# A quad of heads attended two slots after its scores, FFN four slots sooner, the batch loop written out

## What is computed

```python
q = proj(query, Wk, bk); k = proj(key, Wk, bk); v = proj(values, Wv, bv)
scores = einsum('bhqd,bhkd->bhqk', q, k) / sqrt(dk)
scores_ = softmax(where(allow, scores, NEG)) * allow          # allow: strictly below the diagonal
distcum = cumsum(scores_, -1); disttotal = sum(scores_, -1)
dist_scores = sqrt(clip((disttotal - distcum) * |i - j|, 0))
total_effect = clip(exp(dist_scores * -softplus(gammas)), 1e-5, 1e5)
attn = softmax(where(allow, scores * total_effect, NEG))
x = layer_norm(query + (attn @ v) @ Wo.T + bo)
x = layer_norm(x + relu(x @ W1.T + b1) @ W2.T + b2)
```

## Time and profile before

| | |
|---|---|
| median of 3 runs | 1689.13 us (1682.05 to 1694.72) |
| the profiled execution | 1691.98 us |
| its span, first to last instruction | 1689.0 us |
| busy: PE, DVE, ACT, POOL | 1506.9, 1122.4, 1023.1, 157.9 us |
| mean granted clock of TensorE | 0.953 |

### The profile page before, as it was taken

One profiled execution on the slowest core, in us unless ns is written; L12 is line 12 of the kernel. 1 busy time (PEld: TensorE's weight loads), 2 busy tenths in 40 slices (PEclk: granted clock), 3 DMA queues, 4 the chain that ended last, 5 costly groups with the idle time before them and its releaser, 6 DMA issues.

```text
span 1689.0 us, 36801 instructions
## 1 busy us (share of the span) xinstructions
PE 1506.9 (89%) x13056; PEld 1251.6 (74%) x13056; DVE 1122.4 (66%) x3828; ACT 1023.1 (61%) x2674; POOL 157.9 (9%) x107
## 2 busy tenths in 40 slices
PE   4374879999998999999998999999999999988986
PEld 3353668887887888778887878778787878777874
DVE  6576785867766676757857676775857676673221
ACT  1485766676666577666766667666756667674221
POOL 6323110100000010100000010100001010000000
PEclk9786979999998999999999999999999999999998
DMA  5555324656565475646565475656557465566875
GB/s 187 194 187 182 125 101 162 237 177 224 176 212 170 172 251 172 230 170 216 190 207 191 157 244 175 225 177 207 194 178 243 156 234 189 199 224 232 292 270 191
DMA packets 81243, 334.54 MB, mean 198 GB/s; under 512 B 10256, under 2 KB 10256, under 8 KB 64272
## 3 DMA queue, kind: packets, MB, share of 16 engines
q1 hardware_dynamic: 81040, 331.92, 57.3%
HBM read 306.72 MB, written 25.17 MB: 196 GB/s over the span
## 4 chain that ended last, share of the span: by engine, by line
PE 65%; DVE 15%; DMA 8%; issue 5%; ACT 3%; POOL 1%; SPq 1%; DVEq 0%; POOLq 0%; ACTq 0%
PE bank L200 19%; PE bank L201 17%; PE bank L202 17%; PE bank L384 5%; DMA out<-rows 4%; PE bank L398 3%; DVE w_sb L938 3%; DMA w_ring<-w_split 3%; DVE w_sb L950 2%; DVE w_sb L961 2%; PE bank L418 1%; DVE s_sb L926 1%; PE bank L408 1%; DVE c_lo L889 1%; DMA w_split<-w_ring 1%
## 5 line engine op out<-in xcount | busy, mean ns | idle before, releaser
L200 PE MATMUL bank<-xt_hi,w_ring 128*128 128x256 f32 x1024 | 298.4, 291 | 1.9 <-ACT h_sb L721 1.9
L201 PE MATMUL bank<-xt_lo,w_ring 128*128 128x256 f32 x1024 | 291.2, 284 | 0.0
L202 PE MATMUL bank<-xt_hi,w_ring 128*128 128x256 f32 x1024 | 290.8, 284 | 0.0
L200 PE MATMUL bank<-w_ring,h_hi 128*128 128x512 f32 x512 | 219.0, 428 | 23.3 <-DMA w_ring<-w_split 14.7
L721 ACT ACTIVATE h_sb<-bank,b_col 128x256 f32<-128x256 f32 x256 | 106.9, 468 | 212.4 <-DVE h_lo L1027 110.1
L201 PE MATMUL bank<-w_ring,h_hi 128*128 128x512 f32 x512 | 206.4, 403 | 0.0
L384 PE MATMUL bank<-qk_sb 32*32 32x256 f32 (+7 forms) x4096 | 174.3, 298 | 35.8 <-DVE m L926 35.4
L662 ACT ACTIVATE p_sb<-w_sb,nm 128x32 f32<-128x32 f32 (+7 forms) x512 | 206.1, 411 | 0.0
L202 PE MATMUL bank<-w_ring,h_lo 128*128 128x512 f32 x512 | 205.8, 402 | 0.0
L200 PEld LDWEIGHTS bank<-xt_hi,w_ring 128*128 128x128 f32 x1024 | 196.8, 192 | 11.8 <-issue 7.2
L201 PEld LDWEIGHTS bank<-xt_lo,w_ring 128*128 128x128 f32 x1024 | 196.9, 192 | 1.9
(11 more groups left out here) (120 smaller groups left out, 3018.8 us busy)
## 6 DMA issues: line engine op xcount, KB each, us to landing
w_ring<-w_split SPq DMA_DIRECT2D x128, 1024.0 KB, 4.9
w_ring<-w_split SPq DMA_DIRECT2D x256, 512.0 KB, 4.1
w_split<-w_ring SPq DMA_DIRECT2D x32, 512.0 KB, 3.9
x_raw<-x_t SPq DMA_DIRECT2D x16, 512.0 KB, 5.6
c_raw<-ctx_t SPq DMA_DIRECT2D x16, 512.0 KB, 6.2
u_sb<-x_rows SPq DMA_DIRECT2D x16, 512.0 KB, 5.4
ring_raw<-w SPq DMA_DIRECT2D x32, 256.0 KB, 3.0
out<-rows SPq DMA_DIRECT2D x16, 512.0 KB, 6.1
```

The costliest lines, as they stand in the source:

```text
L200: nc.tensor.matmul(dst, a_hi, b_hi, start=start, stop=False)
L201: nc.tensor.matmul(dst, a_hi, b_lo, start=False, stop=False)
L202: return nc.tensor.matmul(dst, a_lo, b_hi, start=False, stop=stop)
```

## The change

Steps are 0 to 18, all written out, with one stage less: in step i the scores of batch i, its attention for quads 0 and 1, the attention of batch i-1 for quads 2 and 3, projection and norm of i-1, and the FFN of i-2 (pairs 0 and 1 of i-1 in slot 3); `done` finishes batch i-3. Quad c goes through `first_exp`, `running_sums` and `effect` in slot c, through `decayed_scores` and `second_exp` in the next, and is attended in the one after that. `s_sb` and `w_sb` have two places, `h_hi` and `h_lo` two each. The weight rings hold four tiles to split, and later two pairs of W1 and two of W2, which is now read back in pairs. The split of the weights takes slots 0 to 5, and its subtraction moves from POOL to DVE. At the start ACT casts wk, wv and wo, DVE subtracts, and POOL casts the first inputs ahead of most constants. SP issues the store of batch i-3 in slot 1 between two of the weight reads, and the rows of the residual after `shift1`. `squared_softplus` moves into slot 0 of step 0.

The diff, cut to the buffers, the orders of ACT and DVE, and slots 1 and 2 of PE:

```diff
-            ring_raw = tensor("ring_raw", [P, 6, 2, 512], F32, loaded)
+            ring_raw = tensor("ring_raw", [P, 8, 2, 512], F32, loaded)
...
-        w_ring = tensor("w_ring", [P, 6, 2, 512], F32R)
+        w_ring = tensor("w_ring", [P, 8, 2, 512], F32R)
...
-        s_sb = tensor("s_sb", [P, NQ, QW])
-        w_sb = tensor("w_sb", [P, NQ, QW])
+        s_sb = tensor("s_sb", [P, 2, QW])
+        w_sb = tensor("w_sb", [P, 2, QW])
...
-        h_hi, h_lo = (tensor(n, [P, 2, S], F32R) for n in ("h_hi", "h_lo"))
+        h_hi, h_lo = (tensor(n, [P, 2, 2, S], F32R) for n in ("h_hi", "h_lo"))
...
-        def over_batches(engine, step):
-
-
-            def plain(i):
-                step(i, i % 2, i < B, 1 <= i <= B, 2 <= i <= B + 1, 3 <= i <= B + 2, 4 <= i, i + 1 < B)
-
-            for i in range(4):
-                plain(i)
-            with engine.Fori(2, B // 2 - 1) as j:
-                step(j * 2, 0, True, True, True, True, True, True)
-                step(j * 2 + 1, 1, True, True, True, True, True, True)
-            for i in range(B - 2, B + 4):
-                plain(i)
-
...
+        def over_batches(step):
+
+
+
+            for i in range(B + 3):
+                step(i, i < B, 1 <= i <= B, 2 <= i <= B + 1, 3 <= i, i + 1 < B)
+
+        def split_in(n):
+
+            return range(3 * n, 3 * n + 3) if n < 4 else range(2 * n + 4, 2 * n + 6) if n < 6 else ()
...
             def first_exp(i, c):
                 act.wait_ge(nm1_ok, NQ * i + c + 1)
-                if not first(i):
-                    act.wait_ge(p_ok, 16 * (i - 1) + HQ * c + HQ)
+                if NQ * i + c >= 2:
+                    act.wait_ge(p_ok, HQ * (NQ * i + c - 1))
...
             def hidden_high(i, p):
                 g = NP * i + p
                 act.wait_ge(h_ok, g + 1)
-                if p > 0 or not first(i):
-                    act.wait_ge(y_step, 2 * g)
-                nc.scalar.copy(h_hi[:], h_sb[:]).then_inc(h_hi_ok, 1)
+                if g >= 2:
+
+                    act.wait_ge(y_step, g - 1)
+                nc.scalar.copy(h_hi[:, p % 2], h_sb[:]).then_inc(h_hi_ok, 1)
...
+            weight_high(0, wk_hi, wk_raw)
+            weight_high(1, wv_hi, wv_raw)
+            act.wait_ge(col_in, 16 * COLS)
+            act.wait_ge(gam_dve, 1)
+            nc.scalar.activation(g_tmp[:, 1], g_tmp[:, 0], ACT.Exp).then_inc(gam_act, 1)
+            weight_high(2, wo_hi, wo_raw)
+            act.wait_ge(const_ok, CONSTS)
+            value_rows(0, 0)
+            over_batches(step)
...
+            def split_low(f):
+                n = f % 4
+                dve.wait_ge(ffw_hi_ok, f + 1)
+                nc.vector.tensor_tensor(w_ring[:, 2 * n:2 * n + 2, 1], ring_raw[:, 2 * n:2 * n + 2, 1],
+                                        w_ring[:, 2 * n:2 * n + 2, 0].bitcast(F32), ALU.subtract).then_inc(ffw_lo_ok, 1)
...
+                if last:
+                    transposes(i - 1, 3, 0)
+                if now:
+                    scores(i, 1, 0)
+                if ffn:
+                    hidden(i - 2, 4)
+                if last:
+                    transposes(i - 1, 3, 1)
+                if now:
+                    scores(i, 1, 1)
+                if last:
+                    transposes(i - 1, 3, 2)
+                if ffn:
+                    add_hidden(i - 2, 3)
+                if now:
+                    scores(i, 1, 2)
+                if last:
+                    attend(i - 1, 3)
+                if now:
+                    pe.wait_ge(v_ok, RT * i + 2)
+                    queries_keys(i, 2)
+                if ffn:
+                    hidden(i - 2, 5)
+                if last:
+                    pe.wait_ge(qk_ok, min(NQ * i + 3, NQ * B))
+                    project_rows(i - 1, 0)
+                if ffn:
+                    add_hidden(i - 2, 4)
+                if now:
+                    transposes(i, 0, 0)
+                    scores(i, 2, 0)
+                if ffn:
+                    hidden(i - 2, 6)
+                if now:
+                    transposes(i, 0, 1)
+                    scores(i, 2, 1)
+                    transposes(i, 0, 2)
+                if last:
+                    pe.wait_ge(u_ok, RT * (i - 1) + 1)
+                    project_rows(i - 1, 1)
+                if ffn:
+                    add_hidden(i - 2, 5)
+                if now:
+                    scores(i, 2, 2)
+                    if last:
+                        pe.wait_ge(u_ok, RT * i)
+                    else:
+                        pe.wait_ge(qk_ok, NQ * i + 3)
+                    queries_keys(i, 3)
+                    attend(i, 0)
+                if ffn:
+                    hidden(i - 2, 7)
+                    add_hidden(i - 2, 6)
+                if last:
+                    turn_rows(i - 1, 0)
...
+                if last:
+                    turned(i - 1, 2, 0)
+                if ffn:
+                    hidden_high(i - 2, 1)
+                    relu(i - 2, 2)
+                if last:
+                    turned(i - 1, 2, 1)
+                    second_exp(i - 1, 3, 0)
+                    turned(i - 1, 2, 2)
+                    second_exp(i - 1, 3, 1)
+                for f in split_in(NQ * i):
+                    split_high(f)
+                if last:
+                    reciprocals(i - 1, 2)
+                if ffn:
+                    hidden_high(i - 2, 2)
+                if last:
+                    concat_high(i - 1, 2)
+                if now:
+                    first_exp(i, 0)
+                    qk_copy(i, 1)
+                if ffn:
+                    relu(i - 2, 3)
+                if done:
+                    deviation2(i - 3)
+                if now:
+                    value_rows(i, 1)
+                    effect(i, 0)
+                if last:
+                    turned(i - 1, 3, 0)
+                if ffn:
+                    hidden_high(i - 2, 3)
+                    relu(i - 2, 4)
+                if last:
+                    turned(i - 1, 3, 1)
+                if now:
+                    second_exp(i, 0, 0)
+                if last:
+                    turned(i - 1, 3, 2)
+                if now:
+                    second_exp(i, 0, 1)
+                for f in split_in(NQ * i + 1):
+                    split_high(f)
+                if last:
+                    reciprocals(i - 1, 3)
+                if ffn:
+                    hidden_high(i - 2, 4)
+                if last:
+                    concat_high(i - 1, 3)
+                if now:
+                    first_exp(i, 1)
+                    qk_copy(i, 2)
+                if ffn:
+                    relu(i - 2, 5)
+                if now:
+                    effect(i, 1)
+                if now:
+                    turned(i, 0, 0)
+                if ffn:
+                    hidden_high(i - 2, 5)
+                    relu(i - 2, 6)
+                if now:
+                    turned(i, 0, 1)
+                    second_exp(i, 1, 0)
+                    turned(i, 0, 2)
+                    second_exp(i, 1, 1)
+                for f in split_in(NQ * i + 2):
+                    split_high(f)
+                if ffn:
+                    hidden_high(i - 2, 6)
+                if last:
+                    deviation1(i - 1)
+                if now:
+                    first_exp(i, 2)
+                    qk_copy(i, 3)
+                    reciprocals(i, 0)
+                    concat_high(i, 0)
+                if ffn:
+                    relu(i - 2, 7)
+                    hidden_high(i - 2, 7)
+                if now:
+                    effect(i, 2)
+                if last:
+                    rows_high(i - 1, 0)
+                if now:
+                    turned(i, 1, 0)
+                    turned(i, 1, 1)
+                if last:
+                    rows_high(i - 1, 1)
+                if now:
+                    second_exp(i, 2, 0)
+                    turned(i, 1, 2)
+                    second_exp(i, 2, 1)
+                for f in split_in(NQ * i + 3):
+                    split_high(f)
+                if now:
+                    reciprocals(i, 1)
+                    concat_high(i, 1)
+                    first_exp(i, 3)
+                if last:
+                    relu(i - 1, 0)
+                    hidden_high(i - 1, 0)
+                if ahead:
+                    qk_copy(i + 1, 0)
+                if last:
+                    relu(i - 1, 1)
+                if now:
+                    effect(i, 3)
+                if ahead:
+                    value_rows(i + 1, 0)
+            weight_high(0, wk_hi, wk_raw)
+            weight_high(1, wv_hi, wv_raw)
+            act.wait_ge(col_in, 16 * COLS)
+            qk_copy(0, 0)
+            act.wait_ge(gam_dve, 1)
+            nc.scalar.activation(g_tmp[:, 1], g_tmp[:, 0], ACT.Exp).then_inc(gam_act, 1)
+            weight_high(2, wo_hi, wo_raw)
+            act.wait_ge(const_ok, CONSTS)
+            value_rows(0, 0)
```

(100 more changed lines are left out.)

647 lines of the change are left out of this document (193 added, 454 removed).

## The result

The changed kernel takes 1736.65 us (median of 4 runs, 1733.75 to 1737.55), the kernel before 1687.41 us in runs beside them (4 runs). The ratio is 1.0299, 95% interval 1.0271 to 1.0326: 3% slower. The forecast was 1715. It had the direction right and the size about half: some 26 us lost (1.5%) were forecast, 49 were measured.

The account below looks back on a forecast made before the run. TensorE was taken to bound the kernel before (91.8 us a batch, 96.2 looped), an ACT and DVE circle the changed one. 190 + 14 x 100.0 - 4 + 68 + 58 = 1712, plus 3: 1715 us, range 1645 to 1758.

Parts of the forecast that it names:

- The circle: Each slot: effect, decayed scores, second exp, first exp, running sums wait in turn across ACT and DVE; at least 18.13 us.
- extras: Other work and waits that the queues put into the circle: 4.6, 6.6, 7.1, 7.9 us in slots 0 to 3.
- The step: One batch in the changed kernel: 98.7 us from the circle, 100.0 with GpSimd and clock; bounds 97 and 103.4.
- GpSimd's 0.6 us: Loss of DVE a step beside GpSimd's input casts and bias add, with one cast meeting running sums.
- no full block: Reading of a scan beside GpSimd's split, 3.77 us against 2.58 alone, used to keep GpSimd's cost at the low end.
- TensorE's idle time: Waits of PE before `attend` in slot 1 and 3 to 4 us at the head of slot 3.
- The 0.7 us: Slot 3: PE's clock drops behind its idle time, later add_hidden and scores move the first exp by this much.
- The head: Stretch up to the first FFN matmul: 190 us against 237.7, bounds 182 and 202.
- The end: Interval to the last batch's FFN 68 us, and last stretch 58 us against 67.5 before.
- The first term: Loop gone and store of `out` issued earlier: at most 4.4 us a batch, 62 us in all.
- rival 3: The circle with 99.5 to 102 us a step, 1707 to 1743 us, slower, the forecast itself; 45%.
- Rival 1: PE stays the bound because the circle fits: 92 to 94 us a step, 1621 us, 4% faster; 10%.

Follow-up runs that it names:

- experiment 2: Changed kernel with `finish_rows` directly behind the running sums of slot 1, ahead of decayed scores, and the store of `out` later in SP's order: 1712.21 us, ratio 1.0143.
- experiment 9: Changed kernel with the orders of TensorE, ScalarE and VectorE rewritten, decayed scores ahead of masks, same operations: 1651.93 us, ratio 0.9781.
- experiment 3: Changed kernel with queries_keys in one pass instead of three, products with the low parts left out: 1727.45 us, ratio 1.0229.
- experiment 4: Changed kernel with GpSimd's add of the bias `bo` cut to 4 elements of a row, so the result lacks `bo`: 1727.12 us, ratio 1.0235.
- Experiment 1: Changed kernel with `finish_rows` moved behind decayed scores and the two masks of slot 1 on DVE: 1723.01 us, ratio 1.0202.
- experiment 10: experiment 9 with slot 3's scores ahead of the FFN's last hidden piece, the second turn_rows behind the last scores, and other moves: 1610.52 us, ratio 0.9545.
- experiment 5: Kernel before with its loop written out and nothing else changed: 1667.29 us, ratio 0.9876.
- experiment 6: Kernel before with its loop written out and the store of `out` issued two pairs earlier in SP's order: 1638.04 us, ratio 0.9697.
- experiment 7: experiment 6 with the start changed: ACT casts weights, DVE subtracts, GpSimd casts inputs before long memsets, TensorE's first projection skips the constants' wait: 1631.36 us, ratio 0.9672.

## Why the prediction was right, and where it was off

**The circle** decided, as the prediction said. Its bare sum of 18.13 us and its extras gave 22.7, 24.7, 25.2 and 26.0 for the slots, before GpSimd and the clock; measured are 22.69, 24.58, 26.27 and 27.60. (The extras listed for slots 2 and 3 add up to 7.0 and 8.0, not 7.1 and 7.9; the two slips cancel.) The start of decayed scores in slot 1, forecast 4.9 us behind `effect`, came at 4.92. Experiments 2 and 9 show it by moving work out of it, experiment 3 by taking TensorE's work away in vain. TensorE is no bystander, though: DVE and ACT wait for it within the circle (0.41 us in slot 0, 2.25 in slot 3, and 2.71 in slot 1 once `finish_rows` is out of the way), and two thirds of what experiment 4 freed went to such a wait. Experiment 1 shows that the count has to follow a moved step to its new place.

**The step** was forecast at 100.0 and took 101.0. The term that was mis-sized is GpSimd's 0.6 us: the rows give 2.3. I had argued that one cast meets running sums; in fact all three operations of a batch meet work of the circle, the casts in slot 2 (1.11 us) and the add in slot 3 (1.15). With them the count gives 26.3 and 27.2 for these slots, against 26.27 and 27.60. The 2.3 is what DVE's own rows lose; removing the add's part brought only 0.4 to 0.5 us a step (experiment 4).

I had also read the row behind this term wrongly, as "no full block". The Trainium skill ("SBUF — State Buffer", SBUF: two separate sides) has the shared port pair held for the whole of an instruction, with the other engine blocked until then. The trace agrees: `hidden_low` ended 0.55 us after the add in fourteen batches of fourteen. In the kernel before, GpSimd's split ran until 60.63 and the scan that began at 59.30 ended 2.43 us after it, about its length alone (2.58). The 1.2 us lost there are the 1.3 us that were left of the split, and not a sign of a milder rule. Nor does the block cost GpSimd's whole 5.1 us a step: what counts is what is left of each operation when one of DVE's begins.

**TensorE's idle time** came where it was said: 1.50 us before `attend` in slot 1 and, at the head of slot 3, more than the 3 to 4 forecast, with the clock at its lower level behind it (1.09 us for a group of four transposes that takes 0.60 to 0.63 at the higher one):

```profile
951.97 0.70 PE L409 MATMUL bank<-zi_wide,head_ones 128*128 128x256 f32 x2 [1.50 <-ACT pt_sb L656]
...
994.32 1.09 PE L399 MATMUL bank<-ident,p_sb 128*128 128x128 f32 x4 [4.90 <-ACT pt_sb L656]
...
1004.71 0.37 ACT L662 COPY cc_sb<-bank 128x256 f32<-128x256 f32 x1 [2.25 <-PE bank L422]
```

It comes back into the circle: ACT then waits 2.25 us for `attend` ahead of the first exp of slot 3, which starts 3.8 us behind the second exp and not 2.9. The 0.7 us that the prediction put down for the clock stands for this wait; how much of it is the clock, no run shows.

**The head** ended at 197.4, not 190. The first `effect` ended at 44.97 (forecast 44.4), so the start was right; the slots behind it were forecast at 21.0, 26.1, 24.0, 22.0, 21.8, 21.4 and took 20.8, 27.4, 23.9, 22.1, 21.8, 27.3. The sixth, 5.9 us longer, is most of the miss. Some 3.1 us of it are GpSimd again: its casts and its add at 180.32 meet the running sums of this slot, whose multiplications take 5.12 us for 2.32 (from 179.43) and the small operation before them 0.55 for 0.23. In experiment 4, without the add, the slot takes 24.0. The rest was not tried apart; in experiment 10, where only the orders differ, the slot is 21.7 and the head 188.4.

**The end** was 71.0 and 55.4, forecast 68 and 58. That the two errors cancel is luck.

**The first term**, 4.4 us a looped step for loop and store, was about right in size and is now split: experiments 5 and 6 take the interval from 96.2 to 94.3 and 91.5 us, and give 22 us to the loop and 29 to the store, 51 in all where the prediction had at most 62. In the changed kernel the loop is gone, and so is the wait for the store.

**The sum** by measured parts: 197.4 + 1411.7 (fourteen intervals) + 71.0 + 55.4 = 1735.5. Against the forecast's 190, 1396, 68 and 58, the step gave 16 of the 24 us and the head 7. So the time fell into the range of rival 3, the forecast, and in its upper half. The forecast loss of 26 us was a small difference of large terms, and 1 us a step, fourteen times, is most of what it was off by.

Rival 1 (TensorE stays the bound, 1621 us) had 10%. It did not come true for the order as written, but that the circle fills a slot is a matter of order, not of the two-slot attention: experiment 10 took 1610.52. From experiment 10 to the changed kernel 126 us are lost by order alone (all four engines' and SP's): 14 x (100.8 - 92.8) = 112, the head 9, the end 5. And the rest of the change pays once the order is right: experiment 10 beats experiment 7, which has the old attention with loop, store and start put right as well, by 20.8 us (one step less: head 41.1 sooner, fourteen intervals of 92.8 against thirteen of 91.5 and 76.3, the end 13 sooner). How much of that is the attention, and how much the FFN's place, the split of the weights or their reads in pairs, was not taken apart.

## What to carry to other kernels

When a dependent operation is moved closer to its producer, add up the whole round of the two engines, with everything that their queues put into it, and compare it with the bound engine's time for the same round: sums of busy time (68 of 101 us here) say nothing about it. In each engine's queue put the operation that closes the round first, put work that is ready in the time in which the other engine has the round, and put no wait for a third engine ahead of it. Before giving a structure up, look for one late transfer: here a store issued two FFN pairs earlier was worth 29 us.

## What the runs showed of the hardware

- The granted clock of TensorE stayed at the higher level (2.4 GHz, 1.00) over 1298.9 us in which it was busy for 99%, with no idle piece above 0.8 us (experiment 10); with pieces of 1.5 and 4.9 us a step it read 0.97 (the changed kernel). A group of four transposes took 0.60 to 0.63 us at the one level and 1.09 at the other.
- An instruction of VectorE that began inside one of GpSimd's ended a fixed time after it: a subtraction that takes 0.69 us alone ended 0.55 us after GpSimd's add in fourteen of fourteen batches, and took 1.20 to 2.79 us. Beside casts of 1.54 and 1.17 us, eight passes of 2.32 us became 3.11 and the small operation before them 0.55 for 0.23. So the loss is about what is left of GpSimd's instruction, and depends on when the other begins.
- A store issued just ahead of the wait for it cost 14 waits, 55.8 us in all; issued two FFN pairs sooner it cost none, and the kernel took 1638.04 us for 1667.29.
